# A two-layer attention and expert kernel: GpSimd's inverse deviation ahead of nine row scatters, and an idle silu activation behind the last exponential

## The reference

```python
def _layernorm(x, axis=-1, eps=1e-05):
    m = jnp.mean(x, axis=axis, keepdims=True)
    v = jnp.var(x, axis=axis, keepdims=True)
    return (x - m) / jnp.sqrt(v + eps)

x = x + _L0_xattn_ref(_layernorm(x), ctx, ctx, mask, ...)
x = x + _L0_ffn_ref(_layernorm(x), ...)          # 32 experts, 8 of them per token
x = x + _L1_xattn_ref(_layernorm(x), ctx, ctx, ...)  # with rotary embedding
x = x + _L1_ffn_ref(_layernorm(x), ...)          # 8 experts, 1 per token, and a shared one

# _L1_ffn_ref, a = 2048 tokens, D = 128, F = 352, E = 8
scores_aE = x_aD @ router_DE
vals_aK, idx_aK = jax.lax.top_k(scores_aE, 1)
gates_Ea = jax.nn.sigmoid(masked_aE).T           # masked: -inf but for the best expert
routed_in_EaD = gates_Ea[:, :, None] * x_aD[None, :, :]
mid_EaF = silu(routed_in_EaD @ w1) * (routed_in_EaD @ w3)
out_aD = silu(x_aD @ ws1) * (x_aD @ ws3) @ ws2 + (mid_EaF @ w2).sum(0)
```

## Time and profile before

| | |
|---|---|
| time, median of 3 runs | 699.15 us (698.3 to 699.52) |
| the profiled execution's own time | 695.65 us |
| its span in the profile | 694.3 us |
| PE busy | 649.7 us, 94% |
| DVE, ACT, POOL busy | 519.4, 400.4, 412.0 us (75, 58, 59%) |
| granted TensorE clock | full in all 40 slices |

### The profile page before, as it was taken

How to read it: one execution, slowest core, us unless ns; L and a number is a source line. 1 busy time by engine, 2 the same in 40 slices (tenths; PEclk the granted TensorE clock), 3 DMA queues, 4 the chain that set the end, 5 groups by cost and what they waited for, 6 DMA issues and landing times.

```text
span 694.3 us, 14218 instructions
## 1 busy us (share of the span) xinstructions
PE 649.7 (94%) x5301; PEld 344.3 (50%) x5301; DVE 519.4 (75%) x934; ACT 400.4 (58%) x567; POOL 412.0 (59%) x613
## 2 busy tenths in 40 slices
PE   5989999999998999999999999999999999898997
PEld 3333433433343566666566543344334343365997
DVE  4798988989988883833645568999988988666454
ACT  2157777778778644332222257777777777654443
POOL 3545558657402255769854575877887743647445
PEclk9999999999999999999999999999999999999999
DMA  5837636743700586486953306546645645104411
GB/s 167 224 96 168 163 101 134 178 113 71 160 2 3 101 201 150 144 173 145 214 134 84 85 24 154 159 135 144 179 152 114 157 100 177 37 25 137 122 33 39
DMA packets 66601, 84.97 MB, mean 122 GB/s; under 512 B 7776, under 2 KB 48624, under 8 KB 65024
## 3 DMA queue, kind: packets, MB, share of 16 engines
q1 hardware_dynamic: 63856, 79.44, 46.2%
q0 software_dynamic: 1760, 3.62, 1.6%
q10 hardware_dynamic: 916, 1.00, 0.6%
HBM read 57.57 MB, written 25.80 MB: 120 GB/s over the span
## 4 chain that ended last, share of the span: by engine, by line
PE 65%; ACT 11%; DMA 6%; DVE 5%; SPq 4%; issue 4%; POOL 4%; ACTq 0%; DVEq 0%; POOLq 0%
ACT prob L918 10%; PE pair L496 10%; PE outs L623 8%; PE pair L357 6%; PE misc L509 6%; PE pair L359 6%; PE pair L358 6%; PE outs L509 5%; PE pair L457 5%; DMA qstack<-mT 4%; DVE negmax L1203 2%; PE misc L410 2%; DMA q_terms<-qparts 2%; SPq L2004 2%; PE outs L395 1%
## 5 line engine op out<-in xcount | busy, mean ns | idle before, releaser
L1203 DVE TENSOR_REDUCE negmax<-pair 128x2 f32<-128x1024 f32 x256 | 306.7, 1212 | 40.0 <-PE pair L457 36.5
L918 ACT ACTIVATE prob<-pair 128x1024 f32<-128x1024 f32 x256 | 259.9, 1024 | 92.0 <-PE pair L496 87.6
L496 PE MATMUL pair<-qstack,kstack 54*128 54x256 bf16 x1024 | 100.4, 274 | 22.5 <-ACT prob L918 19.2
L457 PE MATMUL pair<-kstack,qstack 51*128 51x512 bf16 (+1 forms) x512 | 98.1, 379 | 1.7 <-issue 0.9
L1437 DVE TENSOR_TENSOR hid<-pair,silu 128x512 f32<-128x512 f32 x68 | 46.6, 687 | 69.2 <-PE pair L359 50.6
L496 PEld LDWEIGHTS pair<-qstack,kstack 54*128 54x128 bf16 x1024 | 29.9, 94 | 127.7 <-ACT prob L918 101.0
L1065 ACT ACTIVATE silu<-pair 128x512 f32<-128x512 f32 x68 | 40.5, 597 | 87.8 <-PE pair L359 85.7
L509 PE MATMUL outs<-prob,vaug 128*32 128x256 f32 x1024 | 83.4, 390 | 0.0
L509 PE MATMUL misc<-prob,vaug 128*32 128x256 f32 x1024 | 81.1, 391 | 0.2
L623 PE MATMUL outs<-hid,down 128*128 128x512 f32 x136 | 70.0, 596 | 0.5 <-POOL hid L1867 0.4
L357 PE MATMUL pair<-xT,eh 128*128 128x512 f32 x136 | 70.3, 517 | 0.0
(11 more groups left out here) (288 smaller groups left out, 1084.8 us busy)
## 6 DMA issues: line engine op xcount, KB each, us to landing
kstack<-k_terms SPq DMA_DIRECT2D x30, 384.0 KB
w_here<-w_rows SPq DMA_DIRECT2D x32, 256.0 KB, 4.8
w_there<-w_rows SPq DMA_DIRECT2D x32, 256.0 KB, 5.4
k_terms<-kparts SPq DMA_DIRECT2D x16, 384.0 KB, 2.7
qstack<-q_terms SPq DMA_DIRECT2D x30, 192.0 KB, 4.8
ctx_nat<-in_ctxT SPq DMA_DIRECT2D x16, 256.0 KB, 3.3
k_terms<-kparts SPq DMA_DIRECT2D x16, 256.0 KB, 3.0
w_nat<-in_L_gu SPq DMA_DIRECT2D x9, 352.0 KB, 3.8
```

What stands on the lines that cost most here:

```text
L457: return nc.tensor.matmul(to, qstack[n % 3][rows, g, qt * P:(qt + 1) * P], kstack[n % 3][rows, g, :], start=True, stop=True)
L496: e = nc.tensor.matmul(bank[m + r][:, k * SQ:(k + 1) * SQ], kstack[n % 3][rows, g, (c + k) * P:(c + k + 1) * P], qstack[n % 3][rows, g, :] ...
L918: nc.scalar.activation(prob[:, quad % 2, 2 * g:2 * g + 2, c:c + 2, :].rearrange("p j c q -> p j (c q)"), pair[t_pair(n, step)][:, :, :], A ...
L1203: nc.vector.tensor_reduce(negmax[:, n % 2, 2 * g:2 * g + 2, qt], pair[score_pair(n, step)][:, :, :], AX.X, ALU.max, negate=True).then_inc( ...
```

## The change

Two edits, both around the end of the last period. GpSimd's ten early scatters are split 1 and 9 around `y_scale(14)` instead of 4 and 6. And ScalarE gets one activation of one element with the silu, which reads `col` and writes a cell that nothing reads; it stands in front of the wait that opens `ffn_1`.

```diff
         x = sbuf("x", [P, TT, D], FP32)
         ident = sbuf("ident", [P, P], FP32)
+        unread = sbuf("unread", [1, 1], FP32)
...
             def ffn_1():
                 n = LAYERS * B - 1
+
+                nc.scalar.activation(unread[:, :], col[0:1, 0:1], ACT.Silu)
                 act.wait_ge(pv_done, 16 * LAYERS * B)
                 shared_silu(0)
...
                     if layer == 1 and b == B - 1:
                         if step == 7:
-                            sort_tokens(range(0, 4))
+                            sort_tokens(range(0, 1))
                         if step == 13:
-                            sort_tokens(range(4, 10))
+                            sort_tokens(range(1, 10))
```

## The result

| | before | changed kernel |
|---|---|---|
| median of the runs made together | 699.34 us (698.3 to 700.25) | 694.85 us (694.0 to 696.93) |
| ratio | | 0.9934, 95% interval 0.9907 to 0.9962 |
| the profiled execution's own time | 695.65 us | 696.93 us |
| its span | 694.3 us | 695.5 us |

The changed kernel is 4.5 us faster.

The account below looks back on a forecast made before the run. TensorE's chain was taken as the bound, with a 2.30 us stall and a 0.69 us wait for hid. Both edits together, limited by GpSimd's queue, gave 1.15 us: 699.15 - 1.15 = 698.0 us, range 696.8 to 699.4.

Parts of the forecast that it names:

- the stall in front of the turning: TensorE before the turning of xn for n = 14: 2.30 us idle, because y_scale(14) is queued behind GpSimd's scatters.
- the wait for hid: TensorE at the second shared unit's down product, 611.01: 0.69 us waiting, traced back to the first silu's table load.
- First step, y_scale(14): On GpSimd, y_scale(14) behind one scatter begins at 594.94; the whole 2.30 us stall goes, last exponential 2.26 earlier.
- Second step, the table load: On ScalarE, the 1.28 us load follows the last exponential, covered by TensorE; first silu comes 3.5 us earlier.
- Third step, the queue: On GpSimd, nine queued scatters hold y_scale(15) until about 607.5: 1.15 us earlier, not 2.95; the table load adds nothing.
- The bounds: Limits of the 1.15 us gain, from y_scale(14) beside VectorE's gx and the scatters' pitch: 0.5 to 1.45 us.
- The lower end of 0.5: If y_scale(14) must wait until VectorE's gx is through, GpSimd ends 0.65 us later and the gain is 0.5.
- The sum: Whole kernel: the 1.15 us gain taken off the 699.15 us median gives 698.0 us, 0.16% less.
- The first (the queue no bound): GpSimd: y_scale(15) runs as soon as its input is there; full 2.95 us gain, 696.2 us; chance 0.08.
- the second (stretched scatters): GpSimd: VectorE's work beside the nine scatters stretches them, making the kernel slower, up to 700.9 us; chance 0.05.
- The third (given back in the tail): Behind 611 us: something outside the engines' chain ends the tail, so the gain is lost; 699.15 us; chance 0.07.
- The fourth: ScalarE: the table load stays on the path or costs more; time still 698.0 us; chance 0.80 together with the forecast.

Follow-up runs that it names:

- e3_cell: Kernel before plus only the declaration of the unread 4-byte cell, no new instruction: 697.39 us, ratio 0.9952 to the kernel before.
- e11_filled: Kernel before plus eight products nobody reads, placed in TensorE's stall before the turning of xn for n = 14: 698.39 us, ratio 0.9969.
- e1_order: Kernel before with only the new scatter order (1 and 9), no idle silu and no cell: 697.93 us, ratio 0.9969.
- e8_seven: Changed kernel with seven instead of nine scatters ahead of y_scale(15), the other two behind it: 693.66 us, ratio 0.9908 to the kernel before.
- e4_again: The changed kernel, unaltered, run again beside the kernel before on the same chip: 696.39 us, ratio 0.994.
- e14_cell288: Kernel before plus a 260-byte cell, moving the buffers behind it by 288 bytes, on the fourth chip: 707.76 us, ratio 0.9966.
- e5_warm: Changed kernel with the idle silu writing into the existing buffer warm, no new cell: 699.03 us, ratio 0.998 to the kernel before.
- e6_cell_order: Changed kernel without the idle silu, keeping the cell and the new scatter order: 695.61 us, ratio 0.9939 to the kernel before.

## Why the prediction was wrong, point by point

**What bounds the kernel.** Right in place: the stall in front of the turning and the wait for hid. Too small in price: I counted the 2.30 us in which TensorE stood still and not what came behind it. The other six profiles with that stall show half clock behind it, for 3.4 us in e3_cell (my expectation for e11_filled had 2.6), and 1.1 to 1.3 us of loss in the four off the fourth chip; I had only before's, in which all 40 slices are at full clock, and that execution was faster than any timed run. That a profile 3.5 us below the median lacked something that the median has was there to be asked.

**First step, y_scale(14).** Right: 594.95 on before's clock, forecast 594.94; no idle time before the turning, the last exponential 2.37 earlier (601.10 less 1.81, against 601.66), forecast 2.26.

**Second step, the table load.** Right: it begins at 602.16, on before's clock 600.35 (forecast 600.4), 0.02 behind the end of the exponential; the one-element activation takes 0.20, as taken. The drain of 1380 ns that the Trainium skill (ScalarE: Activation LUTs, "What ACT_TABLE_LOAD costs") puts with the load isn't seen: the next activation starts 0.02 behind it.

**Third step, the queue.** Right: y_scale(15) at 607.45, forecast 607.5, directly behind the ninth scatter; the pitch of the scatters is (608.26 - 599.36) / 7 = 1.27. The gain of the stretch is 1.24 against 1.15, and e1_order has the same without the table load. e8_seven shows the bound from the other side: take two scatters away and 1.67 comes.

**The bounds.** y_scale(14) beside VectorE's gx took 0.23 and 0.72, as it did alone, and began 0.10 behind its input. No lock is seen of the kind that the Trainium skill (SBUF — State Buffer, on the shared port pair) describes for a VectorE instruction in its two-port mode; whether gx runs in that mode, no row shows. The lower end of 0.5 was not reached.

**The sum. This is the step that failed.** It had 1.15 and nothing else. Of the 4.5 (3.8 in e4_again), the declaration of the cell gives about 2.8 (e3_cell; e14_cell288 2.6), the order 1.24 by the traces, and the stall's lower clock some of the rest, since it goes with the stall: e1_order, e5_warm and e11_filled, the three that lose the stall and keep the addresses, are 2.3, 1.5 and 1.9 below before. Without any share of the clock these add up to 4.0, and with the largest of the three to 5.1; measured are 4.5 and 3.8, each to about 2 us. The line `unread = sbuf("unread", [1, 1], FP32)` stands in the diff that the prediction had read out part by part, and the prediction doesn't speak of it: it was costed at nothing because it issues nothing.

**The rivals.** The first (the queue no bound) and the second (stretched scatters) fell with the rows above. The third (given back in the tail) can't be told: behind the down product the changed kernel's profile takes 0.63 more than before's, and the others off the fourth chip from nothing to 1.1 more. The five with nine scatters between the two y_scale take 0.65 more in the mean, the eight others 0.25; with single profiles that scatter by 0.4, that is no difference, but it doesn't rule one out. The fourth, that the table load moves nothing, held, and with it goes e6_cell_order, which has no idle silu and all of the gain.

**The range** reached to 696.8, which none of the cases but the first rival went below. It lacked a case for things that change the time without changing an instruction of the stretch.

**Open.** The first scatter again starts 0.88 behind row_of (594.04 + 0.17 to 595.09); I don't know for what. How the 2.8 divide among the buffers is known only roughly, and about 1.2 of them are in no stretch that the profiles show. Why the cost of the stall differs from run to run, and why the fourth chip takes 10 us more, no run tells.

## What to carry to other kernels

A declaration is part of a change: work out which buffers it moves, and to what address modulo 256, before costing the instructions. When TensorE stands still for two microseconds, look for half clock behind it in more than one profile, and count with it (here 1.1 to 1.3 us) even if the one at hand doesn't show it; before summing on a profile, ask what the median has that the profile lacks. Where an engine's queue takes over from a removed wait, as nine scatters did here, the next gain is in the length of that queue (two scatters fewer: 1.67 us).

## What the runs showed of the hardware that was not expected

Transfers into buffers that begin at a multiple of 256 bytes land sooner: 512 KB in 4.3 to 4.6 us instead of 5.0 to 5.3, and the whole kernel, in which TensorE is busy for more than nine tenths of the time, gains 0.3 to 0.5% by it.

TensorE's clock fell to half behind an idle time of 1.8 to 2.3 us in six of seven profiles. Before's own profile, with 2.30 us idle, is the seventh. So it is not certain in one execution and shows only over several.

Early in the kernel, at 43 to 56 us, the clock varies from profile to profile in kernels with and without the change. The window of 48 to 52 us of e3_cell:

```profile
48.00:52.00 4.00, 4.00 (x24) 1.61 (x20) 1.60 (x3) 1.81 (x2) 0.16 (x1) 0.50 0.47 159
```

By the traces this costs 0.7 to 3.8 us in 15 of the 18 profiles, and nothing in those of before, of the changed kernel and of e6_cell_order. It comes behind short waits of TensorE for ScalarE's first exponentials (0.34, 0.48 and 0.90 us in a row; busy for 2.48 of the 4 us from 40 to 44 in e3_cell). But these are in all 18 profiles, with and without the fall, so what decides it is open, and no run has filled these waits. In the timed executions of before, the mean granted clock goes with 40 to 72% of the variance of the time, by chip; in which stretch the clock was low there is not on record.
